# A gated MLP with per-sequence LoRAs: tiles of 512 tokens in place of 256, one PSUM bank each for gate and up, and the down LoRA's rows multiplied inside the 96-row chunk

## The reference

```python
def lora_add(base, inp, A, B):            # SCALE = 0.5, rank 16
    t = einsum('bri,bni->bnr', A[0][idx], inp)
    return base + einsum('bor,bnr->bno', B[0][idx], t) * SCALE
gate = lora_add(x @ W_gate.T, x, A_gate, B_gate)        # 512 -> 1376
up   = lora_add(x @ W_up.T,   x, A_up,   B_up)
act  = silu(gate) * up
down = lora_add(act @ W_down.T, act, A_down, B_down)    # 1376 -> 512
s    = max(abs(down), 1e-5) along the features
out  = x + ((down / s) @ W_2bit.T) * (s * weight_scale) + bias   # W in -1.5..1.5
```

## Time and profile before

| | us |
|---|---|
| median of 3 runs | 966.07 (965.07 to 967.91) |
| span of the profiled execution | 963.2 |
| PE busy | 926.2 (96%), 6426 matmuls |
| DVE, ACT, POOL busy | 473.5, 337.6, 117.3 |

### The profile page before, as it was taken

One profiled execution on the slowest core, in us unless ns is written; L12 is line 12 of the kernel. 1 busy time (PEld: TensorE's weight loads), 2 busy tenths in 40 slices (PEclk: granted clock), 3 DMA queues, 4 the chain that ended last, 5 costly groups with the idle time before them and its releaser, 6 DMA issues.

```text
span 963.2 us, 21495 instructions
## 1 busy us (share of the span) xinstructions
PE 926.2 (96%) x6426; PEld 860.0 (89%) x6426; DVE 473.5 (49%) x1268; ACT 337.6 (35%) x778; POOL 117.3 (12%) x188
## 2 busy tenths in 40 slices
PE   4799999999999999999999999999999999999994
PEld 4799998999999999999999999999999999999993
DVE  3776345363543636345363643536354363634533
ACT  2545233242423425243242423325243242423421
POOL 0110200111010110200111020110200111020100
PEclk9999999999999999999999999999999999999998
DMA  4672212121121112212111121212212111221010
GB/s 135 196 203 58 63 40 58 36 54 44 47 61 37 53 34 58 58 42 58 36 53 43 50 61 37 58 26 61 55 44 58 36 52 42 52 61 36 23 33 25
DMA packets 56679, 54.83 MB, mean 57 GB/s; under 512 B 20080, under 2 KB 41968, under 8 KB 56656
## 3 DMA queue, kind: packets, MB, share of 16 engines
q1 hardware_dynamic: 55056, 52.08, 20.7%
q10 hardware_dynamic: 1600, 2.49, 0.8%
HBM read 46.14 MB, written 8.39 MB: 57 GB/s over the span
## 4 chain that ended last, share of the span: by engine, by line
PE 86%; DVE 5%; issue 3%; DMA 2%; SPq 2%; ACT 1%; DVEq 0%; ACTq 0%
PE ps_down L1207 24%; PE ps_up L1110 23%; PE ps_gate L1110 22%; PE ps_misc L1238 6%; PE ps_td L1189 4%; DVE b_split L829 2%; PE ps_gate L1145 2%; PE ps_up L1145 2%; PE ps_misc L1229 1%; DMA rows<-w_2bit 1%; DVE act_full L932 1%; ACT act_full L688 1%; DVE wgu L807 1%; DMA ad_raw<-pair_masks 1%; DMA rows<-w_down 0%
## 5 line engine op out<-in xcount | busy, mean ns | idle before, releaser
L1207 PE MATMUL ps_down<-wd,act_split 128*128 128x512 f32 (+1 forms) x1056 | 272.9, 394 | 0.0
L1110 PE MATMUL ps_up<-xs,wgu 128*128 128x256 f32 x1920 | 259.7, 284 | 0.0
L1110 PE MATMUL ps_gate<-xs,wgu 128*128 128x256 f32 x1920 | 258.4, 285 | 0.0
L1110 PEld LDWEIGHTS ps_gate<-xs,wgu 128*128 128x128 f32 x1920 | 248.8, 191 | 9.1
L1110 PEld LDWEIGHTS ps_up<-xs,wgu 128*128 128x128 f32 x1920 | 244.7, 192 | 1.3
L943 DVE TENSOR_TENSOR act_full<-ps_up,act_full 128x256 f32<-128x256 f32 x160 | 67.7, 423 | 309.7 <-PE ps_up L1145 309.7
L1207 PEld LDWEIGHTS ps_down<-wd,act_split 128*128 128x128 f32 (+1 forms) x1056 | 185.9, 188 | 31.1
L696 ACT ACTIVATE act_full<-ps_gate 128x256 f32<-128x256 f32 x160 | 60.5, 378 | 283.4 <-PE ps_gate L1145 283.4
L628 ACT ACTIVATE b_split<-b_raw 64x256 fp32r<-64x256 f32 (+1 forms) x176 | 70.2, 407 | 115.2 <-PE ps_up L1145 115.2
L707 ACT ACTIVATE act_split<-act_full 128x256 fp32r<-128x256 f32 (+1 forms) x176 | 73.1, 415 | 88.9 <-DVE act_full L943 84.1
L829 DVE TENSOR_TENSOR b_split<-b_raw,b_split 32x256 fp32r<-32x256 f32 (+1 forms) x176 | 86.9, 500 | 5.3 <-ACT b_split L628 0.4
(11 more groups left out here) (90 smaller groups left out, 684.1 us busy)
## 6 DMA issues: line engine op xcount, KB each, us to landing
rows<-x_tok SPq DMA_DIRECT2D x128, 64.0 KB, 1.7
x_raw<-x_feat SPq DMA_DIRECT2D x124, 64.0 KB, 1.7
out<-rows SPq DMA_DIRECT2D x124, 64.0 KB, 1.6
b_raw<-b_rows SPq DMA_DIRECT2D x64, 92.0 KB, 2.9
b_raw<-b_rows SPq DMA_DIRECT2D x64, 80.0 KB, 2.5
rows<-w_gu SPq DMA_DIRECT2D x8, 512.0 KB, 4.1
rows<-w_down SPq DMA_DIRECT2D x9, 256.0 KB, 4.2
bd_raw<-b_rows SPq DMA_DIRECT2D x64, 32.0 KB, 1.7
```

Of the source, the lines that this page charges most:

```text
L1110: last = nc.tensor.matmul(ps_out[0:m, f % 2, 0:TILE], w, xs[:, xp, k, :], start=(start and k == 0), stop=(stop and k == KC - 1))
L1207: last = nc.tensor.matmul(ps_down[:, s, :], act_split[0:w, ap, f % 2, s * P:(s + 1) * P], wd[0:w, wp, f, :], start=(f == 0 and n == 0), st ...
```

## The change

In the pair program a tile has 512 tokens (16 sequences), so 8 tiles instead of 16. All its matmuls of gate, up, LoRA and down LoRA stream 512 columns, a whole bank. The general program stays at 256 tokens. The flag now asks for at most one change of LoRA in 16 sequences (`WENTRIES`) instead of 8.

- **PSUM.** `pw_down` has 4 banks, `pw_td`, `pw_gate`, `pw_up` and `ps_misc` one each. Gate of chunk f+1 waits for the silu of chunk f, up of chunk f+1 for the product of chunk f. Chunk 1's gate goes to `ps_misc`, and in the first tile its up to the fourth bank of `pw_down`.
- **Down LoRA.** The masked `t` of the down LoRA stands in rows 96 to 127 of chunk 0's activations (`wact_first`), the LoRA's second factor in rows 96 to 127 of chunk 0's down weights. `wide_first_down` multiplies chunk 0 last, in the next tile, with all 128 rows; the separate `lora_b_down` is gone. Chunk 0's LoRA for gate and up goes straight into the banks, so the copies and sums of `copy_first_gate`, `copy_first_up`, `add_first_lora` are gone.
- **Buffers.** `x` of a tile comes in two halves, `x_raw` and `x_more`. The output is written over the rows that held the scaled down result. The residual gets the bias on POOL (`bias_residual`), and one VectorE instruction (`wide_output`) makes the output.
- **Mask.** The down LoRA's mask is loaded by `end_of`, after all of the earlier tile's stores have landed.

```diff
-            def lora_b_down(tile, pair):
-                pe.wait_ge(bd_ready, tile + 1)
-                pe.wait_ge(td_ready, tile + 1)
...
+            def wide_pass(bank, f, g, n):
+                ws, xp = PASSES[n]
+                for k in range(KC):
+                    w = wgu_first[:, ws, k, g, :] if f == 0 else wgu_chunk(ws, f)[:, k, g, :]
+                    last = nc.tensor.matmul(bank, w, wxs[:, xp, k, :], start=(n == 0 and k == 0), stop=False,
+                                            skip_group_check=(f == 0))
+                return last
...
+            def wide_first_down(tile):
+                pe.wait_ge(bd_ready, tile + 1)
+                pe.wait_ge(td_ready, tile + 1)
+                for s in range(WSUBS):
+                    for n, (ap, wp) in enumerate(PASSES):
+                        last = nc.tensor.matmul(pw_down[:, s, :], wact_first[:, ap, s * P:(s + 1) * P],
+                                                wd[:, wp, 0, :], start=False, stop=(n == 2))
+                    last.then_inc(blocks_done, 1)
...
+                for f in range(2, FC):
+                    if first:
+                        pe.wait_ge(wgu_lo, f + 1)
+                    pe.wait_ge(silu_done, FC * tile + (1 if f == 2 else f))
+                    wide_main(pw_gate[:, :], f, 0)
+                    pe.wait_ge(b_lo, FC * tile + f + 1)
+                    wide_lora(tile, pw_gate, f, 0, gate_done)
+                    pe.wait_ge(act_done, FC * tile + (1 if f == 2 and first else f))
+                    wide_main(pw_up[:, :], f, 1)
+                    wide_lora(tile, pw_up, f, 1, up_done)
+                    if f == 2:
+                        wide_lora_a_down(tile, 0)
+                    wide_lora_a_down(tile, f - 1)
+                    wide_down(tile, f - 1, first)
...
+                def end_of(tile):
+                    sp.wait_ge(stored, 16 * WENTRIES * tile)
+                    sp.wait_ge(td_masked, tile)
+                    load_mask(tile, mask_d, mask_d_in)
...
+            def wide_td_mask(tile):
+                dve.wait_ge(td_copied, tile + 1)
+                nc.vector.tensor_tensor(td_full, pw_td[0:PAIR, :], td_low, ALU.add).then_inc(td_summed, 1)
+                dve.wait_ge(td_summed, tile + 1)
+                dve.wait_ge(mask_d_in, 16 * (tile + 1))
+                nc.vector.tensor_tensor(td_full, td_full, mask_d, ALU.mult).then_inc(td_masked, 1)
+            def wide_td_lo(tile):
+                dve.wait_ge(td_hi, tile + 1)
+                nc.vector.tensor_tensor(wact_first[FIRST_WIDTH:P, LO, :], td_full,
+                                        wact_first[FIRST_WIDTH:P, HI, :].bitcast(F32), ALU.subtract
+                                        ).then_inc(td_ready, 1)
...
+            def wide_program():
+                for e in range(1, ENTRIES, 2):
+                    load_x_entry(act, wide_place(0, ENTRIES + e), x_more[:, e, :], x_more_in)
+                wide_tile(0, True)
...
-                now = ps_plan[32:33, :].rearrange("p (t e) -> p t e", e=ENTRIES)[:, :, 0:ENTRIES - 1]
+                now = ps_plan[32:33, :].rearrange("p (t e) -> p t e", e=WENTRIES)[:, :, 0:WENTRIES - 1]
```

More of the change, by code:

```diff
@@ L118, in build @@
[L118 to L124, removed]
+        rows = sb("rows", [P, 6, H])
+        bias = sb("bias", [P, H])
+        wscale = sb("wscale", [P, 1])
+        ones = sb("ones", [P, 1])
+        amax = sb("amax", [P, WSUBS])
+        rinv = sb("rinv", [P, WSUBS])
+        ascale = sb("ascale", [P, WSUBS])
@@ L196, in build @@
         xres_in = sem("xres_in")
+        wxres_in = [sem(f"wxres{n}_in") for n in range(2)]
+        late_res_in = sem("late_res_in")
         wgu_in = [sem(f"wgu{n}_in") for n in range(2)]
@@ new lines, in wide_residual @@
+            def wide_residual(tile, s, dst, done, behind=False):
+                entries = [entry_at(sp, wide_place(tile, SUB_ENTRIES * s + e)) for e in range(SUB_ENTRIES)]
+                if behind:
+                    sp.wait_ge(out_ready, WSUBS * tile + s - 1)
+                for e in range(SUB_ENTRIES):
+                    sp.dma_start(dst[e * SEQ:(e + 1) * SEQ, :], x_tok[bass.ds(entries[e], 1), :, :]
+                                 .rearrange("a t n -> (a t) n")).then_inc(done, 16)
@@ new lines, in wide_lora, with wide_first_chunk @@
+            def wide_lora(tile, bank, f, g, done):
+                w = WIDTHS[f]
+                nc.tensor.matmul(bank[0:w, :], wb_split[0:STACK, f % 2, g, 0:w], wt_split[0:STACK, g, :],
+                                 start=False, stop=True, skip_group_check=(f == 0)).then_inc(done, 1)
+            def wide_first_chunk(tile, first):
+                if not first:
+                    pe.wait_ge(act_done, FC * tile)
+                else:
+                    pe.wait_ge(wgu_lo, 1)
+                pe.wait_ge(x_hi, 2 * tile + 2)
+                pe.wait_ge(a_ready, tile + 1)
+                for n in range(2):
+                    wide_pass(pw_gate[:, :], 0, 0, n)
+                    wide_pass(pw_up[:, :], 0, 1, n)
+                pe.wait_ge(x_lo, 2 * tile + 2)
+                wide_pass(pw_gate[:, :], 0, 0, 2).then_inc(t_done, 1)
+                wide_pass(pw_up[:, :], 0, 1, 2).then_inc(t_done, 1)
@@ new lines, in wide_lora_a_down @@
+            def wide_lora_a_down(tile, f):
+                w = WIDTHS[f]
+                pe.wait_ge(ad_ready, FC * tile + f + 1)
+                pe.wait_ge(act_lo, FC * tile + f + 1)
+                for part in ((HI, LO) if f == 0 else (LO, HI)):
+                    m = 2 * PAIR if part == HI else PAIR
+                    last = nc.tensor.matmul(pw_td[0:m, :], wad_split[0:w, f % 2, 0:m], wact(part, f),
+                                            start=(f == 0 and part == HI), stop=(f == FC - 1 and part == HI))
+                last.then_inc(td_done, 1)
@@ new lines, in wide_down @@
+            def wide_down(tile, f, first):
+                if first:
+                    pe.wait_ge(wd_lo, f + 1)
+                elif f == 1:
+                    pe.wait_ge(drained, WSUBS * tile)
+                for s in range(WSUBS):
+                    for n, (ap, wp) in enumerate(PASSES):
+                        last = nc.tensor.matmul(pw_down[:, s, :], wact(ap, f)[:, s * P:(s + 1) * P],
+                                                wd[:, wp, f, :], start=(f == 1 and n == 0), stop=False)
+                last.then_inc(down_done, 1)
```

1315 lines of the change are left out of this document (861 added, 454 removed).

## The result

The changed kernel takes **936.91 us** (median, 936.31 to 938.23, 4 runs) against 965.57 (964.97 to 967.91, 4 runs, one more than in the table of the kernel before): a ratio of 0.970, 95% interval 0.968 to 0.971. The forecast was 921 us, range 907 to 936: the sign is right, the gain 29 us instead of 45, just outside the range. The profiled span is 934.9 us, not 918.0.

The account below looks back on a forecast made before the run. PE, busy 96%, was taken as a row of matmuls bound by the distance between starts. Tile 1's start at 122.3, 7 x 109.9 = 769.3 of loop and 26.4 of end gave 918.0; plus 2.9, 921 us, range 907 to 936.

Parts of the forecast that it names:

- Step (a): Steady tile: 286 gate, up and LoRA matmuls of 512 columns replace twice as many of 256, 3.5 us less.
- like `down`, 0.232, or a little worse: Rival for the steady tile: long mains stand 0.232 us apart like `down`, 11 us more, 932; chance 0.15.
- (b) to (d): Steady tile: down LoRA's first factor saves nothing, four `lora_b_down` matmuls go (0.9 us less), chunk 2's LoRA-row wait goes (0.7 less).
- the single banks: Loop: one PSUM bank each for gate and up; silu comes 3 us early, product has the same cover; costed at nothing.
- the x split: Tile's end: splitting `x` needs 2 x 1.06 us after the last up, hidden by about 0.9 under 2 + 12 matmuls.
- The down LoRA's chain: ACT and DVE work before chunk 0's down matmuls, nearly even with PE's arrival; adds 0.2 us a tile (0 to 0.6).
- The start: Before the loop: PE starts at 24.3 after 6.5 us idle, low clock costs 2.0 us, tile 1 starts at 122.3.
- The end: After the loop: bare down LoRA chain, four `ffn` blocks, output and stores, 26.4 us in all.
- two stores on each queue: Kernel's end: two stores a queue without index loads between, 5.9 us from last output to end instead of 7.5.
- The time around the span: Whole run: the median lies 2.9 us over the profiled span, taking 918.0 to 921.
- The weighed rule: Matmul spacing: the skill page's 216 ns for 512 columns would save 25 us more than counted; the rows' 0.227 was kept.
- the rival built on nearly free weight loads: Steady tile: long mains hide the weight load wholly, within 0.003 of 0.213 us, 25 us less, 896; chance 0.05.

Follow-up runs that it names:

- e6: Changed kernel with 32 bytes ahead of `wxs` and 896 more ahead of `wact_first`, all matmul operands at 128 modulo 256: 919.11 us.
- e7: e1 with 78 dummy matmuls at the start instead of 24: 927.82 us.
- e1: Changed kernel with one unused tensor of 32 bytes a partition ahead of the wide tensors: 927.56 us.
- e12: e6 with `x_more` loaded ahead of the indices and, in the first tile, masks and splits of `t` ahead of the LoRA second factor's split: 917.09 us.
- e11: e12 with 66 dummy matmuls at the start instead of 24: 915.32 us.
- e5: Changed kernel with 160 bytes a partition ahead of `wxs`, putting `wxs` at 0 and `wact_split`, `wdt_split` at 128 modulo 256: 929.67 us.
- e2: Changed kernel with 32 bytes ahead of `wxs` and 32 behind it, so only `wxs` and nearby small buffers move onto 64-byte lines: 929.01 us.
- e10: e6 with `wxs` and the small LoRA buffers behind it 64 bytes further, `wxs` at 192 modulo 256: 924.72 us.
- e9: Kernel before with four small tensors allocated ahead of `x_raw`, so `xs`, `act_split` and `dt_split` lie at 0 modulo 256: 966.52 us, ratio 1.001.
- e3: Kernel before with one unused tensor of 32 bytes a partition ahead of `x_raw`: 962.54 us, ratio 0.996.
- e8: e7 with SyncE's four `x_more` loads ahead of its LoRA index loads, and 66 dummy matmuls instead of 78: 926.68 us.

## Why the prediction was off, step by step

- **Step (a), the failed one.** "286 x (0.239 - 0.227) = 3.5 us less" was mis-sized: the 512-column mains stood at 0.2325 to 0.233, so the step gave 286 x 0.006 = 1.7 us, and the 32 `ffn` matmuls a tile, taken as unchanged at 0.227, gave back 32 x 0.007 = 0.2. Together, with distances good to 0.001, that is the 1.9 us a tile by which the loop was longer, 13 us in all. The rival "like `down`, 0.232, or a little worse" (932) described the outcome, with the wrong reason: it spoke of alternating data and banks, and e6 takes the mains back to 0.227 with neither changed. e6 shows the cause, the addresses. With the operands where the kernel before had them, step (a)'s 0.227 holds for mains and `ffn` alike, and 919.11 us is within 2 of the forecast. Part of that closeness is luck: `down` at 0.228 in place of the forecast's 0.232 gives 1056 x 0.004 = 4 us that nobody had counted on, and the end takes 1.5 more than forecast. The step was sound for the addresses of the kernel before, and I had not looked whether the addresses stay equal. The order of the allocations in the change shows that they don't.
- **(b) to (d), the single banks, the x split: nothing speaks against them.** There is no wait of PE in the loop, and the separate `lora_b_down` is gone.
- **The down LoRA's chain: as near as forecast.** In the kernel after it costs nothing (the forecast took 0.2 us a tile). In e6, where PE gets there sooner, its list of waits has none in the loop either (two waits of 0.6 us that the kernel after doesn't have lie in its first tile).
- **The start: first main 24.73 (forecast 24.3), clock loss 2.9 us (forecast 2.0).** The forecast took the one low stretch of the earlier trace rows, 3.4 us long; here the matmuls stood 0.43 to 0.46 us apart until about 30.9, some 6 us. e7 shows that e1, whose chunk 0 was slow too (7.4 us), gets nothing back from the clock by itself, since the split of `t` came no sooner; e12 and e11 show that it does once that wait is moved.
- **The end: 28.3 (forecast 26.4).** The times up to the last output hold: chunk 0's multiplication at T + 4.2 (forecast 4.3), the first `ffn` at T + 9.3 (9.5; the row at 915.94), the last output ready at T + 20.0 (20.5), where T = 906.63. Inside them two errors cancel. The first `ffn` was to run at half speed with 3.45 us; it took 2.13, and the granted clock was 1.00 from 907 to 928. And the blocks were to follow at 1.8 to 2 us; the rows of `ffn` start at 915.94, 918.86, 921.77 and 923.74, so two of the three steps are 2.9. What failed is "two stores on each queue": ScalarE's 8 stores stand behind all of its arithmetic, the first is issued at 922.78 and they take 1.0 us each, so the last leaves at 930.8, 4.1 us after its rows were ready; from the last output to the end there are 8.3 us instead of 5.9. No run tried another division of the stores.
- **The time around the span** was 2.0 us, not 2.9. The 2.9 set the median of three runs beside the span of another run; the runs of the kernel before lie 1.8 us over their own spans. These 0.9 us, counted too many, made the forecast look better than its span was: 16.9 us off in the span, 15.9 in the time.
- **The weighed rule.** The Trainium skill, page "TensorE: Matmul & The Clock Gate", section "Back-to-back issue gap", puts an isolated matmul of 512 columns at 216 ns. The best that any kernel here shows in a row is 0.227, as in the row of `ffn` of e6. The trace again does not agree, and the rival built on nearly free weight loads (896) is not reached even at the best addresses.

## What to carry to other kernels

When a change adds or resizes a small tensor, compare the addresses of all matmul operands before and after: a distance between matmuls taken from the old trace held here only while the streamed operand and the weights loaded beside it kept their places modulo 256 bytes. If a matmul that the change did not touch gets slower, look there first; here one unused tensor was worth 9.4 us and two 17.8. And a stall or slow stretch that is removed at the start paid here only once what stands behind it (the split of `t`) moved too.

## What the runs showed of the hardware

- 512-column fp32 matmuls in a row stood 0.227 to 0.2285 us apart when streamed operand and loaded weights both lay at 128 modulo 256 (e6, all three kinds; e5, `ffn` and `down`; e2, the mains; e1, the mains of up), 0.229 to 0.231 when they lay 64 bytes apart (e10), 0.2325 at 128 apart (e1, e5, e9), and 0.2325 to 0.234 with one operand 32 bytes off a 64-byte line (after, e2, e3). Whether 128 itself or the equality counts is open, and what inside the chip does this no run here tells.
- Two things don't fit. `down` in the kernel before stood at 0.232 with both operands at 128. And gate stood above up in e1 (0.230 against 0.2275) and in e10 (0.231 against 0.229), though both stream `wxs` and load `wgu`; in e1 `ffn` and `down` were slow beside it, in e10 they were not.
- 256-column matmuls didn't pay it: 0.119 at 128 bytes' difference (e9), 0.117 to 0.118 at 32 bytes off the line (e3), 0.1196 before. A long matmul beat two short ones by 0.012 us at good addresses (0.227 against 0.239), and by nothing at those of e3 (0.234 against 0.233 to 0.236).
- The granted clock was 0.50 from 24.73 to 28.20, behind 6.6 us without a matmul, and 1.00 when dummy matmuls filled that time (e11). A shorter wait can be enough: in e8 PE waited 2.03 us and the clock was 0.50 from 37.15 to 40.50; in e7 it waited 2.45 us and the clock stayed at 1.00.
